# Four heads of a scan side by side in four column groups of TensorE, with the output already in channels

## The reference

```
z, x, B, C, dt = split(rmsnorm(h) @ w_in_proj)          # z, x: 256 channels; B, C: 8 heads x 64
x  = silu(conv(x));  dt = softplus(dt @ w_dt + b_dt), mean over the 32 channels of a head
l  = cumsum(dt * A)                                     # within a chunk, for each head
y  = (mask * exp(l_t - l_i) * (C_t . B_i)) @ x          # within the chunk
   + exp(l_t) * C_t @ state                             # from the chunks before
state = exp(l_last) * state + sum_i exp(l_last - l_i) * B_i x_i
y  = (y + x * D) * silu(z)
out = residual + rmsnorm(y) * w_norm_out @ w_out_proj
```

## Time and profile before

| | |
|---|---|
| median of three runs | 759.35 us (758.93 to 760.9) |
| the profiled execution | 760.49 us |
| its span in the trace | 758.4 us |
| busy: TensorE matmul, weight load | 656.0 us (86%), 514.7 us (68%) |
| busy: VectorE, ScalarE, GpSimd | 477.1 us (63%), 359.9 us (47%), 176.7 us (23%) |
| mean granted TensorE clock | 0.946 of full |

### The profile page before, as it was taken

One profiled execution on the slowest core, in us unless ns is written; L12 is line 12 of the kernel. 1 busy time (PEld: TensorE's weight loads), 2 busy tenths in 40 slices (PEclk: granted clock), 3 DMA queues, 4 the chain that ended last, 5 costly groups with the idle time before them and its releaser, 6 DMA issues.

```text
span 758.4 us, 11829 instructions
## 1 busy us (share of the span) xinstructions
PE 656.0 (86%) x3890; PEld 514.7 (68%) x3890; DVE 477.1 (63%) x1148; ACT 359.9 (47%) x837; POOL 176.7 (23%) x249
## 2 busy tenths in 40 slices
PE   4477869989889988989889988999989988988896
PEld 3355857677767766777767766777767766776664
DVE  6654266566766587467767587467767587465544
ACT  3624136634564346644655346544655346542252
POOL 7146110323013210323014110323014110232002
PEclk9879579999999999999999999999999999999799
DMA  7000000000000000000000000000000000000000
GB/s 230 8 15 2 1 0 1 15 1 1 0 29 1 1 1 1 29 1 1 0 28 0 0 0 8 20 0 0 0 28 0 0 1 15 1 1 0 15 1 14
DMA packets 12345, 8.89 MB, mean 12 GB/s; under 512 B 1259, under 2 KB 10902, under 8 KB 12310
## 3 DMA queue, kind: packets, MB, share of 16 engines
q1 hardware_dynamic: 12310, 8.44, 3.6%
HBM read 6.34 MB, written 2.10 MB: 11 GB/s over the span
## 4 chain that ended last, share of the span: by engine, by line
PE 49%; DVE 24%; issue 6%; ACT 5%; POOL 0%; DVEq 0%; POOLq 0%; ACTq 0%
PE bank L485 7%; PE bank L360 6%; PE bank L362 5%; PE bank L361 5%; PE bank L464 4%; PE bank L562 4%; PE bank L563 3%; PE bank L564 3%; DVE act_l L1105 3%; PE bank L478 2%; PE bank L473 2%; ACT decay L781 2%; DVE cv L933 2%; PE bank L506 1%; PE bank L441 1%
## 5 line engine op out<-in xcount | busy, mean ns | idle before, releaser
L757 ACT ACTIVATE act_h<-bank 128x512 fp32r<-128x512 f32 x192 | 116.8, 609 | 205.2 <-PE bank L362 203.2
L1105 DVE SCALAR_TENSOR_TENSOR act_l<-bank,act_h 128x512 fp32r<-128x512 f32 x192 | 131.2, 687 | 117.3 <-ACT act_h L757 115.3
L360 PE MATMUL bank<-fTl,w1h 128*128 128x512 f32 x192 | 92.2, 480 | 22.1 <-DVE fTl L1060 11.2
L1299 POOL TENSOR_TENSOR late<-late 128x512 f32<-128x512 f32 x32 | 41.4, 1293 | 259.7 <-DVE late L1113 259.7
L781 ACT ACTIVATE decay<-bank,lneg 128x128 f32<-128x128 f32 x256 | 71.2, 382 | 35.4 <-PE bank L441 35.4
L562 PE MATMUL bank<-act_l,w2h 128*128 128x512 f32 x192 | 80.1, 417 | 3.7 <-DVE act_l L1105 2.2
L563 PE MATMUL bank<-act_h,w2l 128*128 128x512 f32 x192 | 78.0, 406 | 0.0
L362 PE MATMUL bank<-fTh,w1h 128*128 128x512 f32 x192 | 77.9, 406 | 0.0
L564 PE MATMUL bank<-act_h,w2h 128*128 128x512 f32 x192 | 77.6, 404 | 0.0
L361 PE MATMUL bank<-fTh,w1l 128*128 128x512 f32 x192 | 77.3, 402 | 0.0
L360 PEld LDWEIGHTS bank<-fTl,w1h 128*128 128x128 f32 x192 | 36.8, 191 | 44.5 <-DVE act_l L1105 32.6
(11 more groups left out here) (193 smaller groups left out, 1258.3 us busy)
## 6 DMA issues: line engine op xcount, KB each, us to landing
x_in<-L_attn_hidden_dram SPq DMA_DIRECT2D x8, 256.0 KB, 2.8
out_dram<-late SPq DMA_DIRECT2D x8, 256.0 KB, 2.8
late<-L_ffn_sw_dram SPq DMA_DIRECT2D x2, 512.0 KB, 6.3
late<-L_ffn_rw_dram SPq DMA_DIRECT2D x1, 1024.0 KB, 6.7
CT<-L_attn_w_in_proj_dram SPq DMA_DIRECT2D x1, 772.0 KB, 4.6
b_dt<-L_attn_b_dt_dram SPq DMA_DIRECT2D x1, 128.0 KB, 3.3
w_out_raw<-L_attn_w_out_proj_dram SPq DMA_DIRECT2D x1, 128.0 KB, 3.5
rows<-L_ffn_sb_dram SPq DMA_DIRECT2D x1, 4.0 KB
```

The source lines that it names most:

```text
L360: mm(dst, stat_h, mov_l, start=True, stop=False)
L757: nc.scalar.activation(act_h[:, b % RING, :], HID[b % 2][:], ACT.Relu).then_inc(act_h_ready, 1)
L1105: v_.scalar_tensor_tensor(act_l[:, r, :], HID[b % 2][:], 0.0, f(act_h[:, r, :]), ALU.max, ALU.subtract)\
L1299: g.tensor_tensor(acc, acc, term, ALU.add).then_inc(acc_ready, 1)
```

## The change

The product within a chunk swaps its operands. The stationary operand is now `xs` of one head (128 tokens x 32 channels) and the moving operand is `mg` with 128 columns. Four heads write the four groups of 32 partitions of one bank region, so the output has channels on partitions. The product with the state does the same with 64 x 64-channel pairs of heads. It adds in PSUM to the same place, so exp(l) must already be in C: `growth_rows` lays out l on TensorE, ScalarE's `growth` takes the exponential, and GpSimd's `grown` multiplies C by it. The state has two buffers, and VectorE does it ahead of y. The skip x * D is one fused step of VectorE on `yT`, which `silu_x` has filled with silu of the convolution in channels. z is projected in channels, dt in pieces of 256 columns. The transposes and their copies are gone. Sums of squares are matmuls of `sq` with a column of ones. `dt_clamp` stands at step 3, `residual` at step 9, and `mean_square` behind `routed_out`. D arrives in eight small transfers in place of one.

```
@@ proj
-                if j in (6, 7, 8, 9):
-                    pe.wait_ge(dtv_ready, nth(s, 4, j - 5))
+                if j in (6, 7):
+                    pe.wait_ge(dtv_ready, nth(s, 2, j - 5))
+                if j in (8, 9):
+                    pe.wait_ge(sz_ready, nth(s, 2, j - 7))
...
+                elif j < 4:
+                    for k in range(2):
+                        c = 2 * (j - 2) + k
+                        ins = split(dst[:, k * DI:(k + 1) * DI], hTh[:, at(c)], hTl[:, at(c)], wh[:, DT0:DT0 + DI], wl[:, DT0:DT0 + DI])
                 elif j < 6:
-                    c = j - 2
-                    ins = split(dst[:], hTh[:, at(c)], hTl[:, at(c)], wh[:, 0:512], wl[:, 0:512])
+                    k = Z0 + (j - 4) * P
+                    ins = split(dst[:], wh[:, k:k + P], wl[:, k:k + P], hTh[:], hTl[:])
@@ segments
                     if c > 0 and hf == 0:
-                        pe.wait_ge(y_steps, nth(s, 10, 1 if c == 1 else 3 * c - 3))
+                        pe.wait_ge(y_steps, nth(s, 8, 2 * c))
@@ y_product
+            def growth_rows(s, c):
+                pe.wait_ge(btok_ready, nth(s, 3, c))
+                for n in range(NP):
+                    ins = mm(TR[:, at(n)], pick_head[:].rearrange("r h l -> r (h l)")[:, 2 * n * P + NS:2 * n * P + NS + P], lT[:, at(c)], start=True, stop=True)
+                ins.then_inc(grow_psum, 1)
...
-                if c > 0:
-                    pe.wait_ge(state_step, nth(s, 8, (2, 5, 8)[c - 1]))
-                    for n in range(NP):
-                        mm(MAIN[0][:, 256 + n * 64:320 + n * 64], CT[:, n, at(c)], state[:, n, :], start=True, stop=True)
...
-                pe.wait_ge(mg_ready, nth(s, 8, 2 * c + 2))
-                for hf in range(2):
-                    for n in range(NP):
-                        h = 2 * n + hf
-                        ins = mm(MAIN[0][:, h * HD:(h + 1) * HD], mg[:, hf, n, :], xs[:, c, h * HD:(h + 1) * HD],
-                                 start=True, stop=True)
+                if c > 0:
+                    pe.wait_ge(state_step, nth(s, 8, (2, 5, 8)[c - 1]))
+                    pe.wait_ge(cte_ready, nth(s, 3, c))
+                for b in range(NB):
+                    if c > 0:
+                        for k in range(2):
+                            n = 2 * b + k
+                            mm(MAIN[0][64 * k:64 * k + 64, at(b)], state[:, (c - 1) % 2, n, :], CTe[:, n, :], start=True, stop=False)
+                    if b == 0:
+                        pe.wait_ge(mg_ready, nth(s, 8, 2 * c + 2))
+                    for q in range(4):
+                        h = 4 * b + q
+                        ins = mm(MAIN[0][HD * q:HD * q + HD, at(b)], xs[:, c, h * HD:(h + 1) * HD], mg[:, h % 2, h // 2, :],
+                                 start=c == 0, stop=True)
                 ins.then_inc(y_psum, 1)
...
+            def sum_squares(s, c):
+                if c == 0 and is_seq(s, n_seq - 1):
+                    pe.wait_ge(grow_ready, nth(s, 3, 3))
+                pe.wait_ge(sq_ready, nth(s, 4, c + 1))
+                for b in range(NB):
+                    ins = mm(TR[:, c:c + 1], sq[:, b, at(c)], ones[:, 0:1], start=(b == 0), stop=(b == NB - 1))
+                if c == NCH - 1:
+                    ins.then_inc(ssq_psum, 1)
@@ scan_part and body of TensorE
                     if step == 1:
-                        if c > 0:
-                            y_transposes(s, c - 1)
                         gram(s, c, prev)
+                        if c < NCH - 1:
+                            growth_rows(s, c + 1)
...
-                    y_transposes(s, NCH - 1)
+                    for c in range(NCH - 1):
+                        sum_squares(s, c)
                     if ahead:
                         proj(s + 1, 1)
+                    sum_squares(s, NCH - 1)
                     out_projection(s)
@@ ScalarE
+            def silu_x(s, b):
+                act.wait_ge(conv_step, nth(s, 8, 4 * b + 4))
...
+                nc.scalar.activation(yT[:, b, :], cv[:, b, :], ACT.Silu).then_inc(xT_ready, 1)
...
+            def growth(s, c):
+                act.wait_ge(grow_psum, nth(s, 3, c))
...
+                nc.scalar.activation(grow[:].rearrange("p n l -> p (n l)"), TR[:], ACT.Exp).then_inc(grow_ready, 1)
+
+            def squares(s, c):
+                act.wait_ge(yz_ready, nth(s, 4, c + 1))
...
+                nc.scalar.activation(sq[:, :, at(c)], yT[:, :, at(c)], ACT.Square).then_inc(sq_ready, 1)
@@ attend, the third step (the state's steps now stand ahead of these)
+                    dve.wait_ge(y_psum, nth(s, 4, c + 1))
...
+                    for b in range(NB):
+                        v_.scalar_tensor_tensor(yT[:, b, at(c)], yT[:, b, at(c)], d_col[:, b:b + 1], MAIN[0][:, at(b)],
+                                                ALU.mult, ALU.add).then_inc(y_steps, 1)
+                    dve.wait_ge(y_steps, nth(s, 8, 2 * c + 2))
+                    v_.tensor_tensor(yT[:, :, at(c)], yT[:, :, at(c)], szT[:, :, at(c)], ALU.mult).then_inc(yz_ready, 1)
@@ scan_part of VectorE
-                if i == 2:
+                if i == 3:
                     dt_add(s, 0)
                     dt_add(s, 1)
-                if i == 3:
-                    dt_add(s, 2)
-                if i == 4:
-                    dt_add(s, 3)
                     dt_clamp(s)
...
+                if i == 9:
+                    residual(s)
@@ GpSimd, behind weigh
-            def skip(s, c):
+            def grown(s, c):
...
+                g.tensor_tensor(CTe[:], CT[:, :, at(c)], grow[:], ALU.mult).then_inc(cte_ready, 1)
```

More of the change, by code:

```diff
@@ L162, in build @@
         xw = sb("xw", [P, NP, 2, HD])
-        xd = sb("xd", [P, DI])
-        state = sb("state", [P, NP, 2 * HD])
+        grow = sb("grow", [P, NP, P])
+        CTe = sb("CTe", [P, NP, P])
+        state = sb("state", [P, 2, NP, 2 * HD])
         state_m = sb("state_m", [P, NP, 2 * HD])
-        yt = sb("yt", [P, DI])
-        yz = sb("yz", [P, DI])
-        junk = sb("junk", [P, DI])
-        ssq = sb("ssq", [P, NCH])
+        sq = sb("sq", [P, NB, SEQ])
         msq = sb("msq", [P, NCH])
@@ L364, in hn_transposes @@
             def hn_transposes(s):
[L365 to L366 removed]
+                if (v := nth(s, 3, 0)) is not None:
+                    pe.wait_ge(grow_ready, v)
                 for c in range(NCH):
@@ L818, in scan_part @@
                         decays(s, c)
-                    if step == 1 and c > 0:
-                        y_out(s, c - 1)
+                    if step == 1:
+                        if c > 0:
+                            squares(s, c - 1)
+                        if c < NCH - 1:
+                            growth(s, c + 1)
                     if step == 2 and c == NCH - 1 and not is_seq(s, n_seq - 1):
```

154 lines of the change are left out of this document (65 added, 89 removed).

## The result

The changed kernel takes 708.2 us (705.91 to 713.26, four runs), the kernel before 759.67 (758.93 to 760.9) beside it. The ratio is 0.933, with a 95% interval of 0.9275 to 0.9385. In six further runs the changed kernel took 711.6 us (707.55 to 715.4).

The account below looks back on a forecast made before the run. TensorE's queue was taken to bound most of the kernel, in places a VectorE step it waits for. 0.0 (TensorE's work) - 23.0 - 2.2 (waits) + 5.6 (VectorE) - 2.0 (first body) = -21.6 us, to 738, range 718 to 769.

Parts of the forecast that it names:

- The product within a chunk and the one with the state: TensorE, per sequence: at 0.068 us a record, 1.09 us a chunk (-2.7 us) and 0.54 with the state (-0.9 us).
- rival 4: Product within a chunk: all four column groups overlap fully, 0.028 us a record, 21 us less, 717; chance 0.10.
- The price of a change: TensorE: 17 changes of the array's division a sequence at 0.10 us each, +1.7 us; bounds 0 and 0.27 each.
- Rival 2: TensorE: each change of division empties the array, 0.27 us, 23 us more in all, 761; chance 0.13.
- rival 1: TensorE's products: column groups run one after another at 0.111 us a record, 30 us more, to 768; chance 0.18.
- Transposes, `growth_rows`, `sum_squares`, projections: TensorE, per sequence: four transpose pairs go, -1.0 us; `growth_rows` +1.0, `sum_squares` at the body's end +1.8, projections +0.1.
- The waits: TensorE in the chunks: waits of `segments` (16.3 us) and for `btok` (8.6) go, 1.9 given back, -23.0 us.
- rival 3: Chunks: the waits come back elsewhere, the product waiting for `mg`; all 23.0 us return, 761; chance 0.10.
- VectorE's opening: VectorE, steps 0 to 3: both double `dt_add` and `dt_clamp` ahead of `fT_low`, +0.8 us in seven bodies, +5.6 us.
- At no cost: GpSimd's products, ScalarE's exponentials, `mean_square`, small transfers and `residual` at step 9 were to cost nothing.
- the first body: No blocks there and the clock at 1.2 GHz from 71 to 103 us: -2.0 us, bounds 0 and -6.
- rival 5: First body: the clock stays at 2.4 GHz since TensorE waits less, 12 us less, 726; chance 0.05.

Follow-up runs that it names:

- after_again: The changed kernel run once more unaltered, as the measure for the kernels run beside it: 711.6 us (707.55 to 715.4).
- b_both_waits: Kernel before, with the state in two buffers and updated ahead of y's steps, and `gram` ahead of y's transposes: 727.34 us, ratio 0.9557.
- a_one_group: Changed kernel, but all eight heads of the product within a chunk write the same 32 partitions, one column group in place of four: 750.71 us.

## Why the prediction was wrong in size

**The product within a chunk and the one with the state: the step that failed.** The prediction read `gram`'s 0.068 us a record as "the two records of one head go to the same place and cannot overlap, the next head's first one can", and took it for four groups as for two. Two things in that were wrong. The four groups overlap fully, and the prediction's 1.09 us a chunk measured 0.58: 16 records without their change take 0.58 - 0.145 = 0.44 us, 0.027 each, which is the prediction's lower bound and rival 4 (717, chance 0.10). And `gram`'s 1.09 us are 0.20 more than two halves fully side by side would take (16 x 0.111 / 2 = 0.89). I put that down to its own change of division, which was not tried alone; if so, taking its pitch and then counting changes as well paid for them twice. Two numbers, 0.107 to 0.111 us for a record within its group and 0.145 for a change, give all four measured times: 4 in series + 1 change = 0.58 (0.58), 2 x 4 in series + 4 changes = 1.45 (1.45), with two changes 1.16 (1.16), and one group, 16 in series + 1 change, 1.86 to 1.92 (1.87). The products and the changes cost -1.9 us a sequence in the prediction and (0.58 - 1.76) + 3 x (1.45 - 2.60) = -4.6 in the trace: 22 us of the miss. The signs that the prediction named for being wrong (a pitch of 0.11 us, a dearer change, a fall of the clock in the chunks) all pointed to a slower kernel, and none of these came; of the waits that it named, only that for `CTe` came, 1.7 us in all.

**The price of a change** was nearly right, 0.145 against 0.10. It fits the changes between 64 and 32 columns and the one back to the whole array. The one from the whole array into the groups costs less: L490, ahead of it, takes 370.89 - 369.96 = 0.93 us where the same matmuls took 418.52 - 417.63 = 0.89 before. Rival 2's 0.27 did not come. The Trainium skill, TensorEngine Tiling (Array Packing), Key Properties, says that changing the mode drains TensorE; that a change costs something agrees with the 0.145 here.

**The skill's sentence for rival 1.** TensorE: Matmul & The Clock Gate, Part 3, of the Trainium skill says that a weight load overlaps a running matmul only when the row group differs. Here all groups share their rows, every record has a load of its own, and four groups still take 0.58 us against 1.87 for one, 3.2 times less with the change in it. The 16 loads take 0.38 us, while the matmuls of the same records run. For column groups the measurement stands against that sentence as I read it. The same part gives 2.38 times for three tiles, with 512 columns. That is 0.79 for each tile, and 3.2 for four is 0.80, so with that figure the trace agrees.

**Transposes, `growth_rows`, `sum_squares`, projections**: -1.0, +1.0, +1.8 and +0.1 forecast. `growth_rows` measured 3 x 0.32 = +1.0, `sum_squares` +1.6, and its experiment confirms that it is paid in full. The transposes were not tried alone, but with them at -1.0 the parts, -4.6 - 1.0 + 1.0 + 1.6 + 0.1 = -2.9, come within 0.1 of the work that one body lost (below).

**The waits**: -23.0 forecast for the kernel; the two changes in the kernel before are worth 25 us at full clock. Right. But the prediction gave the reordering of state and y its value for the wrong kernel: in the changed one it is worth about 2 us, since y's steps have become short by themselves. No new wait for `mg` came (rival 3), and the one for `CTe` is 1.7 us in all, in the first body. The wait of 0.32 us for `act_low` at a body's end (-2.2 forecast) went, but the `second` blocks now wait 3.5 us more for `late`, 0.42 in a body; the prediction has no term for that.

**VectorE's opening**: +0.8 us a body forecast. From the first step of the network's opening on VectorE (L1059, before L1038) to `fTl` it is 340.79 - 328.67 = 12.1 us now and was 365.51 - 354.34 = 11.2, so +0.9. The clamp alone is 0.72. Right, with one difference: the prediction looked for `fT_low`'s waits to grow to 17 us. They fell to 7.4, and the projection's wait for `dtv` took 12.3. Together they are 19.7, and before they were 11.2 + 2.5 = 13.7: 6.0 more, against 5.6 forecast.

**"At no cost"**: `residual`, which stood behind `l_parts` in step 10, was to delay `l_parts` at step 9 "by what it no longer delays `gT_copy`". That is what happened. TensorE's wait for `gT` went, 7.8 us in all and 1.11 in a body, and a wait for `l_parts` of 0.94 in each of seven bodies came, 6.7 us. What the prediction missed is that neither wait has to be paid: with `residual` at step 12 both are gone, and the body is 1.0 us shorter.

**One body, waits and work apart.** In the full-clock body of the kernel before (from 268.01 us) TensorE's idle times add up to 7.88 us, in one of the changed kernel (from 326.52) to 5.87. The waits for the state (2.29), `btok` (0.61), `gT` (1.11) and `act_low` (0.32) are gone. Those for `lparts` (0.94), `late` (0.42) and y (0.28) are new, and `dtv` and `fTl` take 1.10 + 0.94 in place of 1.37. So the waits give 2.0 us of the 84.18 - 79.35 = 4.83, and the other 2.8 are less work in the queue, where the prediction had 0.0.

**Outside the full-clock bodies: a term that was too small.** Eight times 4.83 us are 38.6, and the median fell by 51.5. The two profiled executions, whose spans differ by 54.2 us, show where the rest lies:

- The first `out_projection` starts at 91.24 us and before at 101.59, 10.35 us earlier, 5.5 more than a full-clock body gives. Most of it is in the third chunk, which takes 75.92 - 66.47 = 9.45 us from one `segments` to the next and took 84.81 - 69.14 = 15.67. The clock falls at about 72 us in both, so most of this chunk ran at the lower clock before and a third of it does now. The prediction had -2.0 for the first body, with bounds of 0 and -6.
- From the first to the last `out_projection` it is 38.8 us less, 5.0 more than seven full-clock bodies give. Three bodies of the kernel before with a low stretch take 85.68, 84.63 and 85.68 in place of 84.18.
- From the start of the last `out_projection` to the end it is 62.61 in place of 67.65 us, another 5.0. Here chance plays a part: in after_again, the same kernel as the changed one, this piece takes 66.5 us, with the clock low from 654 to 665 us.

At 0.946 of a span of 758.4 us, the kernel before lost 41 us to the low clock; at 0.969 of 704.2 us, the changed one lost 22, and in its other executions, down to 0.955, up to 32. These are upper bounds, since TensorE does not set the pace everywhere. The prediction let the clock play a part in the first body alone (rival 5) and took the low stretches in the middle and the 20 us at 0.66 near the end as given.

Do the waits within the chunks pull the clock down? Two of the five low stretches of the kernel before began within a microsecond behind a wait for the state, the one shown here and one that ended at 593.75:

```profile
423.47 0.39 PE L441 MATMUL bank<-lT,pick_head 24*128 24x128 bf16 x4 [1.23 <-DVE state L1023]
```

With the state's wait taken out the median clock rose from 0.949 to 0.964, and with waits put into the changed kernel it fell from 0.960 to 0.953. Against it, the stretches around 240 and 506 us had no wait in the timeline in the 6 us ahead of them, and with both waits out b_both_waits still had two in the middle. So the waits have a part in it, and what else makes the clock fall, and what share of the 12.9 us is the clock's at all, stays open.

**The account.** The forecast was -21.6 us. The work in the bodies gave 8 x 2.82 = 22.6 us more gain. The waits gave 3.5 less: 8 x 2.01 = 16.1 in place of 23.0 + 2.2 - 5.6 = 19.6. What lies outside the full-clock bodies gave 12.9 in place of 2.0, 10.9 more. -21.6 - 22.6 + 3.5 - 10.9 is -51.6, as measured; but the 12.9 is itself what is left over beside the eight full-clock bodies.

Rival 1 (groups in series, 768) is close to what a_one_group builds, though there the product with the state keeps its two groups. It takes 39 to 43 us more than the changed kernel. Its full-clock body, 84.15 us, is as long as that of the kernel before, 84.18; its time is only 1.3% below (ratio 0.9866, 0.9789 to 0.9943), and 5 us of that stand ahead of the first `out_projection` (96.62 against 101.59 us). So without the groups side by side the change gains nothing in a full-clock body.

## What to carry to other kernels

- Before the pitch of a small group of matmuls is carried to another shape, take out what it pays once (the change of division). Compare two runs of the same records that differ in one of the two: here one group against four (1.87 and 0.58 us) gave the pitch, and four changes against two (1.45 and 1.16 us) gave the price of a change. With one pitch for both, the changes are counted twice.
- A step that leaves one queue's critical place lands ahead of something else. "It delays B by what it no longer delays A" may be an even trade, as here 0.94 us for 1.11, and still not the best place: look for one behind both. Here 1.0 us a body and 0.72 us a body were got back by moving two VectorE steps behind what TensorE waits for.
- Where executions differ by the granted clock, compare one repeated body at full clock. It showed 0.2 us where the medians could not show 4. Then look at what lies outside those bodies: here a quarter of the gain was there.

## What the runs showed of the hardware that I had not expected

- Four column groups of 32, each with its own weight load for each record, work fully side by side: 0.027 us a record of 128 columns in float32, against 0.11 in one group, and the order of the heads doesn't matter (0.59 against 0.58 us).
- A change of the array's division costs about 0.145 us between 128 x 64 and 128 x 32 groups, and about 0.04 from the whole array into the groups.
- Executions of one and the same kernel differ by 7 to 8 us with the granted clock (705.91 us at 0.969 and 713.26 at 0.958; 707.55 at 0.968 and 715.4 at 0.955), more than most single edits here. The kernel before varied less, 758.5 to 763.57 us at 0.942 to 0.951 in all its runs. One stretch of 11 us at the lower clock, from 654 us, made the last piece of the changed kernel 66.5 us long in place of 62.6.
